# Pair 0 of a mixed, clamped low-rank linear layer as the plain product of four weight blocks

## The chip, the core and the metric

The kernel runs on one core of one Trainium2 chip. The metric is the device time of one execution in microseconds (us), as a median of several runs. TensorE (PE, with its weight loads as PEld) multiplies matrices, VectorE (DVE), ScalarE (ACT) and GpSimd (POOL) work elementwise, and SyncE (SP) and ScalarE issue the transfers (DMA) that appear here. SBUF is the memory on the chip, PSUM the banks in which TensorE sums.

## The reference

What is computed, with all inputs in float32:

```python
# x (128, 64, 1024), ids (128,), cond_w (16, 64, 64), W (1024, 1024), b (1024,)
# A (8, 1024, 16), Bm (8, 16, 1024), p (8,)
y = einsum('bct,bcd->bdt', x, cond_w[ids])          # one of 16 mixers for each batch row
z = einsum('bsd,od->bso', y, W) + b
u = einsum('bsd,edr->ebsr', y, A)
m = einsum('ebsr,ero,e->bso', u, Bm, p)
gamma = minimum(0.5 * norm(z) / (norm(m) + 1e-6), 1.0)   # norms over the last axis
return x + z + gamma * m
```

## The kernel before

Two batch rows of 64 channels fill the 128 partitions, which gives 64 tiles of 128 rows by 1024 columns, taken in 32 **pairs** (tile 2p is "r = 0", tile 2p + 1 is "r = 1"). The transposed W lies in four blocks of 512 by 512: W11 and W12 take the lower half of a tile's 1024 inputs, W21 and W22 the upper half, to the lower (1) or upper (2) half of the outputs.

**Precision.** Every operand of a large product is split in a high part (`..._hi`, a cast on ScalarE) and the rest (`..._lo`, a subtraction on VectorE), and a product of a tile half with a block is 4 chunks of 128 inputs times 3 passes (hi·hi, hi·lo, lo·hi): 12 matmuls of 512 columns. A "product" below means these 12.

**Seven products in place of eight.** For two tiles, four half-tile inputs and four blocks the plain way takes eight products. The kernel takes seven, by Strassen's scheme in Winograd's form: it needs sums of the inputs (S1 to S4, from the mixed tiles) and of the blocks:

```python
T1 = W12 - W11;  T2 = W22 - T1;  T3 = W22 - W12;  T4 = W21 - T2
```

T1 to T4 are made once, at the start, and split like W; W11, W21 and W22 are needed as they are. The results are put together again on VectorE with the bias (`bias_p1`, `make_u2`, `make_u3`, `make_z11`, `make_z12`, `make_z22`).

**What a pair is on TensorE**, in the steady loop (`step` at the end of the kernel): product W11 into bank b_ps; `down` (24 matmuls of 256 columns, the low-rank u); W21 onto b_ps, after `p1_biased`; `up(0)` (the low-rank m of tile 0); T4 into a_ps; T2 into b_ps; the next pair's tile 0 mixed (`mix`, with the mixers); T1 into c_ps; T3; the next tile 1 mixed; `up(1)`; W22 onto c_ps. The order on each engine is written out by hand; semaphores (`wait_ge`, `then_inc`) tie the engines together.

**Pair 0 before the change.** TensorE's order is the 12 warm-up matmuls on zeros (L818); mix tile 0; W11; mix tile 1; W21; `down`; T2; T1; T3; mix tile 2; W22; T4; mix tile 3; `up(1)`; and then pair 1 with W11. GpSimd makes S1, S4, the difference of the biases, and in chunks T1 (L350) and T3 (L355). VectorE makes T2 (L542) and T4 (L546) from them, one chunk after the other, and all the `_lo` parts of W (L535), y (L554), S (L575) and A (L654). ScalarE makes the `_hi` parts of W (L395), y (L400) and S (L413).

**Loads.** All are on SP's queue, in this order: ids, x tile 0, the two mixer squares of tile 0 (64 by 64 each, at an address read from the ids), W11 in 4 chunks, x tile 1, the mixers of tile 1, bias, W21, A, W12, W22, p, B, x tiles 2 and 3, and the mixers of these.

Of the kernel before, what the change touches and what calls it, by code (L numbers as in the profile page):

```python
# [5 lines left out]
def conditioned_clamped_low_rank_linear_kernel(  # L6
# [10 lines left out]
):  # L17

# [30 lines left out]
    W_ORDER = (W11, W21, T2, T1, T3, W22, T4)  # L49
# [7 lines left out]
    RAW11, RAW21, RAW12, RAW22 = range(4)  # L57
    w_blocks = [w[h * H:(h + 1) * H, o * H:(o + 1) * H].rearrange("(k p) o -> k p o", p=P)
                for h, o in ((0, 0), (1, 0), (0, 1), (1, 1))]

    ctx = ExitStack()
    with ctx:  # L62
# [45 lines left out]
        def stat(n, r):  # L108
# [6 lines left out]
        raw11 = w_hi_raw[:, T4, :, :]  # L115
        raw21 = w_lo_raw[:, T4, :, :]
        raw12 = w_lo_raw[:, T3, :, :]
        raw22 = w_lo_raw[:, W22, :, :]
        raw = [raw11, raw21, raw12, raw22]
        w_from = {W11: raw11, W21: raw21, W22: raw22, T3: raw12, T4: raw21,  # L120
                  T1: w_lo_raw[:, T1, :, :], T2: w_lo_raw[:, T2, :, :]}
# [15 lines left out]
        w_loaded = [[sem(f"w_loaded{n}_{k}") for k in range(HC)] for n in range(4)]  # L137
# [11 lines left out]
        w_lo_ready = sem("w_lo_ready")  # L149
        t1_made = sem("t1_made")  # L150
# [21 lines left out]
        u3_biased = sem("u3_biased")  # L172
# [55 lines left out]
        def _(sp):  # L228
# [13 lines left out]
            sp.dma_start(cond_ids[:, :], condition.rearrange("(o n) -> o n", o=1)).then_inc(ids_loaded, 16)  # L242
# [53 lines left out]
        def _(pool):  # L296
            def make_s1(p):

                pool.wait_ge(s2_made, p + 1)
                nc.gpsimd.tensor_tensor(s14[:, 0, :, :], s23[:, 0, :, :], s14[:, 0, :, :], ALU.add).then_inc(s1_made, 1)  # L300

            def make_s4(p):

                pool.wait_ge(s2_made, p + 1)
# [42 lines left out]
            for k in range(HC):  # L347
                pool.wait_ge(w_loaded[RAW11][k], 16)
                pool.wait_ge(w_loaded[RAW12][k], 16)
                nc.gpsimd.tensor_tensor(w_from[T1][:, k, :], raw12[:, k, :], raw11[:, k, :], ALU.subtract  # L350
                                        ).then_inc(t1_made, 1)
            for k in range(HC):
                pool.wait_ge(w_loaded[RAW22][k], 16)
                pool.wait_ge(t1_made, k + 1)
                nc.gpsimd.tensor_tensor(raw12[:, k, :], raw22[:, k, :], raw12[:, k, :], ALU.subtract  # L355
                                        ).then_inc(t3_made, 1)
# [26 lines left out]
        def _(act):  # L383
# [553 lines left out]
```

## Time and profile before

| | |
|---|---|
| median of 3 runs | 952.65 us (952.53 to 954.38) |
| the profiled execution: its own time | 954.46 us |
| the profiled execution: span of the core | 952.6 us |
| TensorE matmuls busy | 918.7 us, 96% of the span |
| VectorE, ScalarE, GpSimd busy | 61%, 38%, 36% of the span |
| granted TensorE clock, mean | 0.983 |

The 1.9 us between the span and the execution's own time lie around the program. "Granted clock" is the share of full speed that TensorE was given: 1.00 is its 2.4 GHz level and 0.50 its 1.2 GHz level. The page gives TensorE's share of each fortieth of the span (23.8 us each). The first fortieth has 6 tenths, the next three 5, 8 and 9, and all the others 9 or more but for the last with 5.

### The profile page before, as it was taken

How to read it: one execution, taken by the hardware profiler on the slowest of the kernel's cores; microseconds unless marked ns; L12 is line 12 of the kernel's file. 1: busy time of each engine (PE TensorE's matmuls, PEld its weight loads, DVE VectorE, ACT ScalarE, POOL GpSimd, SP SyncE). 2: the span in 40 equal slices, each digit the busy share in tenths (PEclk: the TensorE clock that was granted, in tenths of full speed). 3: DMA queues.
4: the chain of work that ended last, by engine and by line, in shares of the span. 5: the costliest groups of instructions: out<-in, count | busy, mean ns of one | idle time of the engine just before them, and what ended most of it. 6: DMA issues, size and time to landing. Idle time of an engine off the chain costs nothing. (4 is left out here: it accounts for less than half of the span.)

```text
span 952.6 us, 15191 instructions
## 1 busy us (share of the span) xinstructions
PE 918.7 (96%) x4876; PEld 789.8 (83%) x4876; DVE 583.6 (61%) x903; ACT 357.7 (38%) x704; POOL 346.1 (36%) x336
## 2 busy tenths in 40 slices
PE   6589999999999999999999999999999999999995
PEld 4478888888888888888888888888888888888883
DVE  4995566665556565556565556666555656555653
ACT  4353343434333434334334334343433343432431
POOL 2623344332244433234433234433224443323442
PEclk8699999999999999999999999999999999999998
DMA  8201222211222221122121122221122222112201
GB/s 260 78 23 69 92 92 69 91 65 48 91 91 76 84 87 47 70 91 91 69 91 45 67 91 91 69 91 67 48 88 91 81 79 90 45 69 91 92 23 66
DMA packets 32457, 75.17 MB, mean 79 GB/s; under 512 B 12729, under 2 KB 13754, under 8 KB 32442
## 3 DMA queue, kind: packets, MB, share of 16 engines
q1 hardware_dynamic: 32442, 74.99, 22.4%
q8 instruction: 7, 0.11, 0.0%
q14 instruction: 8, 0.07, 0.0%
HBM read 41.42 MB, written 33.55 MB: 79 GB/s over the span
## 5 line engine op out<-in xcount | busy, mean ns | idle before, releaser
L400 ACT CAST y_hi<-mix_ps 128x512 fp32r<-128x512 f32 x128 | 75.7, 591 | 322.9 <-PE mix_ps L739 322.9
L331 POOL TENSOR_TENSOR stats<-stats 128x1 f32<-128x1 f32 x32 | 17.7, 554 | 447.1 <-ACT squares L447 447.1
L575 DVE TENSOR_TENSOR s_lo<-s,s_hi 128x512 fp32r<-128x512 f32 x128 | 142.1, 1129 | 4.9 <-ACT s_hi L413 0.6
L317 POOL TENSOR_TENSOR z<-z,x_in 128x512 f32<-128x512 f32 x64 | 82.7, 1293 | 130.4 <-ACT squares L428 130.4
L739 PEld LDWEIGHTS mix_ps<-mixer,x_in 128*128 128x128 f32 x1024 | 124.0, 191 | 5.9 <-issue 1.0
L739 PE MATMUL mix_ps<-mixer,x_in 128*128 128x128 f32 x1024 | 124.6, 275 | 0.5 <-DMA mixer<-in_L_cond_weights_dram 0.5
L413 ACT CAST s_hi<-s 128x512 fp32r<-128x512 f32 x128 | 79.0, 618 | 114.3 <-POOL s L305 96.5
L554 DVE TENSOR_TENSOR y_lo<-mix_ps,y_hi 128x512 fp32r<-128x512 f32 x128 | 87.9, 687 | 53.9 <-ACT s L406 48.6
L752 PE MATMUL b_ps<-w_hi,y_hi 128*128 128x512 f32 x256 | 102.1, 399 | 7.9 <-DVE z L640 4.8
L752 PE MATMUL b_ps<-w_hi,s_hi 128*128 128x512 f32 x256 | 100.5, 392 | 9.4 <-DVE w_lo L535 9.4
L752 PE MATMUL c_ps<-w_hi,s_hi 128*128 128x512 f32 x256 | 102.4, 400 | 1.9 <-issue 1.8
L752 PE MATMUL b_ps<-w_lo,y_hi 128*128 128x512 f32 x256 | 101.3, 396 | 0.0
L752 PE MATMUL b_ps<-w_hi,y_lo 128*128 128x512 f32 x256 | 101.1, 395 | 0.0
L752 PE MATMUL b_ps<-w_lo,s_hi 128*128 128x512 f32 x256 | 100.3, 392 | 0.0
L752 PE MATMUL b_ps<-w_hi,s_lo 128*128 128x512 f32 x256 | 100.1, 391 | 0.0
L752 PE MATMUL c_ps<-w_lo,s_hi 128*128 128x512 f32 x256 | 99.8, 390 | 0.0
L752 PE MATMUL c_ps<-w_hi,s_lo 128*128 128x512 f32 x256 | 99.8, 390 | 0.0
L620 DVE TENSOR_TENSOR z<-b_ps,z 128x512 f32<-128x512 f32 x32 | 22.1, 692 | 111.6 <-PE b_ps L752 111.6
L707 DVE TENSOR_TENSOR z<-a_ps,bias 128x512 f32<-128x512 f32 x31 | 21.4, 692 | 107.2 <-PE a_ps L752 107.2
L311 POOL TENSOR_TENSOR z<-z,x_in 128x1024 f32<-128x1024 f32 x32 | 76.8, 2402 | 0.0
L785 PE MATMUL u_ps<-y_hi,a_hi 128*128 128x256 f32 x256 | 73.4, 287 | 0.6 <-DVE a_lo L654 0.6
L785 PE MATMUL u_ps<-y_lo,a_hi 128*128 128x256 f32 x256 | 73.3, 286 | 0.0
(92 smaller groups left out, 1835.7 us busy)
## 6 DMA issues: line engine op xcount, KB each, us to landing
x_in<-in_x_dram SPq DMA_DIRECT2D x64, 512.0 KB, 3.6
out_dram<-z SPq DMA_DIRECT2D x64, 512.0 KB, 2.7
w_lo_raw<-in_L_ffn_W_dram SPq DMA_DIRECT2D x12, 256.0 KB, 7.2
mixer<-in_L_cond_weights_dram SPq DMA_DIRECT2D x128, 16.0 KB, 2.1
w_hi_raw<-in_L_ffn_W_dram SPq DMA_DIRECT2D x4, 256.0 KB, 3.7
bias<-in_L_ffn_b_dram SPq DMA_DIRECT2D x1, 512.0 KB, 5.0
a_lo_raw<-in_L_ffn_A_dram SPq DMA_DIRECT2D x1, 512.0 KB, 7.3
b_lo_raw<-in_L_ffn_B_dram SPq DMA_DIRECT2D x1, 512.0 KB, 7.9
```

The lines of the kernel that those rows point to most:

```text
L311: nc.gpsimd.tensor_tensor(z1[:, :], z1[:, :], x_in[:, slot, :], ALU.add).then_inc(residual1_ready, 1)
L317: nc.gpsimd.tensor_tensor(z0[:, par, cols], z0[:, par, cols], x_in[:, 2 * par, cols], ALU.add).then_inc(residual0_ready, 1)
L331: nc.gpsimd.tensor_tensor(stat(NORM_Z, 1), stat(Z_SQ, 1), half, ALU.pow).then_inc(norm_z_ready[1], 1)
L400: nc.scalar.copy(y_part(y_hi, r, h), mixed(h)).then_inc(y_hi_ready, 1)
L413: nc.scalar.copy(s_hi[:, n, :, :], s_raw(n)).then_inc(s_hi_ready, 1)
L554: nc.vector.tensor_tensor(y_part(y_lo, r, h), mixed(h), y_part(y_hi, r, h).bitcast(fp32), ALU.subtract).then_inc(y_lo_ready, 1)
L575: nc.vector.tensor_tensor(s_lo[:, n, :, :], s_raw(n), s_hi[:, n, :, :].bitcast(fp32), ALU.subtract).then_inc(s_lo_ready, 1)
L620: nc.vector.tensor_tensor(z1[:, up_], b_ps[:, :], z0[:, par, up_], ALU.add).then_inc(u3_ready, 1)
L707: nc.vector.tensor_tensor(z1[:, lo], a_ps[:, :], bias[:, 2, :], ALU.add).then_inc(p4_biased, 1)
L739: made = nc.tensor.matmul(mix_ps[:, h, k * P:(k + 1) * P], x_in[:, slot, (h * HC + k) * P:(h * HC + k + 1) * P], mixer[:, r, :], start=Tru ...
L752: summed = nc.tensor.matmul(bank[:, :], left[:, k, :], right[:, n, k, :], start=(start and k == 0 and i == 0), stop=(k == HC - 1 and i == ...
L785: summed = nc.tensor.matmul(u_ps[:, 0:2 * P], left[:, k, :], right[:, k, :], start=(k == 0 and n == 0), stop=(k == KC - 1 and n == 2))
```

## The change

Pair 0 is no longer computed with seven products, but with the eight plain ones, straight from W11, W12, W21 and W22, which all have their splits made as they arrive. The new function `plain` runs one of them for tile r and half h, and counts in `plain_done`. Tile 0 goes to b_ps and c_ps, tile 1 to a_ps and the first half of m_ps. S1 to S4 of pair 0 and their splits are gone, and so is the recombination: VectorE adds the bias to four banks.

T1 to T4 are first used in pair 1. VectorE makes all of them, in instructions of 1024 columns (two chunks, `chunks`), in the order T3, T1, T2, T4, with the four bias additions between them; their splits (`split_t`) are of 1024 columns too, in the order T4, T2, T1, T3, and stand in VectorE's and ScalarE's order among the work on pair 0's end and pair 1's inputs. GpSimd keeps the difference of the biases and nothing else of that.

The ids and the mixers of tiles 0 and 1 are issued by ScalarE, ahead of its first cast. SP issues x tiles 0 and 1, then W11, W12, W21, A, W22, bias, p, B, x tiles 2 and 3, and only then waits for the ids, for the mixers of tiles 2 and 3. GpSimd clears the mixers before the zeros of the warm-up. The loop from pair 2 on is the same but for counts that start one lower.

```diff
@@ SP
-            sp.dma_start(cond_ids[:, :], ...)
-            sp.dma_start(x_in[:, 0, :], x_tiles[0]).then_inc(x_loaded[0], 16)
-            sp.wait_ge(ids_loaded, 16)
-            sp.wait_ge(mixer_zeroed, 1)
-            load_mixer(0, 0)
-            load_w(RAW11)
-            sp.dma_start(x_in[:, 1, :], x_tiles[1]).then_inc(x_loaded[1], 16)
-            load_mixer(1, 1)
+            for r in range(2):
+                sp.dma_start(x_in[:, r, :], x_tiles[r]).then_inc(x_loaded[r], 16)
+            load_w(W11)
+            load_w(W12)
+            load_w(W21)
+            sp.dma_start(a_raw, ...)
+            load_w(W22)
@@ GpSimd
-            make_s1(0)
-            make_s4(0)
...
-            for k in range(HC):
-                nc.gpsimd.tensor_tensor(w_from[T1][:, k, :], raw12[:, k, :], raw11[:, k, :], ALU.subtract
-            for k in range(HC):
-                nc.gpsimd.tensor_tensor(raw12[:, k, :], raw22[:, k, :], raw12[:, k, :], ALU.subtract
@@ ScalarE
+            act.dma_start(cond_ids[:, :], ...)
+            act.wait_ge(ids_loaded, 16)
+            act.wait_ge(mixer_zeroed, 1)
+            for r in range(2):
+                load_mixer(r, r)
...
+            split_w(W22)
+            square_z11(0, 0, True)
             split_u(0, True)
+            split_t(T4)
             act.wait_ge(bm_scaled, 1)
             nc.scalar.copy(b_hi[:, :], b_raw).then_inc(b_hi_ready, 1)
+            for h in range(2):
+                split_y(2, 0, h)
+                copy_y(1, h, True)
+            split_t(T2)
+            for h in range(2):
+                split_y(3, 1, h)
+            square_z1(0, True)
+            split_t(T1)
+            square_m1(0, True)
+            split_t(T3)
@@ VectorE
+            def make_t3():
+                for g in range(2):
+                    nc.vector.tensor_tensor(chunks(raw_t[T3], g), chunks(raw22, g), chunks(raw12, g), ALU.subtract
+                                            ).then_inc(t3_made, 1)
...
+            make_t3()
+            dve.wait_ge(plain_done, 5)
+            nc.vector.tensor_tensor(z0[:, 0, lo], b_ps[:, :], bias[:, 0, :], ALU.add).then_inc(z11_ready, 1)
+            make_t1()
+            dve.wait_ge(plain_done, 6)
+            nc.vector.tensor_tensor(z1[:, lo], a_ps[:, :], bias[:, 0, :], ALU.add).then_inc(z21_ready, 1)
+            make_t2()
+            make_t4()
...
+            split_t(T4)
...
+            split_y(1, 0, 0)
+            dve.wait_ge(plain_done, 8)
+            nc.vector.tensor_tensor(z1[:, up_], m_ps[:, lo], bias[:, 1, :], ALU.add).then_inc(z22_ready, 1)
+            split_y(1, 0, 1)
+            split_t(T2)
             split_y(1, 1, 0)
-            make_s3(1, False)
+            make_s3(1, True)
             split_y(1, 1, 1)
-            make_s2(1, False)
+            make_s2(1, True)
+            split_t(T1)
+            split_t(T3)
@@ TensorE
+            def plain(bank, r, h, n):
+                product(bank, y_part(y_hi, r, h), y_part(y_lo, r, h), n, h == 0, h == 1, r == 0, True
+                        ).then_inc(plain_done, 1)
...
+            for r, bank in ((0, b_ps[:, :]), (1, a_ps[:, :])):
+                y_ready(r, 0)
+                plain(bank, r, 0, W11)
+            for r, bank in ((0, c_ps[:, :]), (1, m_ps[:, lo])):
+                plain(bank, r, 0, W12)
+            for r, bank in ((0, b_ps[:, :]), (1, a_ps[:, :])):
+                y_ready(r, 1)
+                plain(bank, r, 1, W21)
             down()
...
+            plain(c_ps[:, :], 0, 1, W22)
+            for h in range(2):
+                mix(0, 2, h)
+            plain(m_ps[:, lo], 1, 1, W22)
             mix_next_1(0, 0, 0)
```

On **VectorE**, from the end of pair 0 to the bias addition that lets TensorE start pair 1's W21 (`bias_p1`, the addition into z from b_ps and bias). Before, w_lo is the low part of a block, y_lo that of a mixed tile, s a sum S2 or S3:

```order
L535 TENSOR_TENSOR w_lo<-w_lo_raw,w_hi 128x512 x4
L679 TENSOR_TENSOR b_lo<-b_lo_raw,b_hi 128x1024
L554 TENSOR_TENSOR y_lo<-mix_ps,y_hi 128x4x128 x2
L683 TENSOR_TENSOR z<-a_ps,z 128x512
L554 TENSOR_TENSOR y_lo<-mix_ps,y_hi 128x4x128
L562 TENSOR_TENSOR s<-s,mix_ps 128x512
L554 TENSOR_TENSOR y_lo<-mix_ps,y_hi 128x4x128
L570 TENSOR_TENSOR s<-mix_ps,s 128x512
L630 TENSOR_TENSOR z<-c_ps,z 128x512
L575 TENSOR_TENSOR s_lo<-s,s_hi 128x512
```

The same place after the change (L587 is the split of a T, L617 that of S2; the three small ones are the clamp's factor, L649 adds the low-rank part of tile 1, L682 is `bias_p1`):

```order
L612 TENSOR_TENSOR s<-mix_ps,s 128x512
L587 TENSOR_TENSOR w_lo<-w_lo_raw,w_hi 128x1024 x4
L617 TENSOR_TENSOR s_lo<-s,s_hi 128x512
L629 TENSOR_SCALAR stats<-stats 128x1
L632 RECIPROCAL stats<-stats 128x1
L635 TENSOR_SCALAR stats<-stats 128x1
L649 SCALAR_TENSOR_TENSOR z<-m_ps,stats,z 128x1024
L682 TENSOR_TENSOR z<-b_ps,bias 128x512
```

The splits of T1 and T3, which stood before pair 0's last products, stand now behind pair 1's S2 and ahead of `bias_p1`.

On **ScalarE**, the first instructions of the program. Before:

```order
L472 ACT_TABLE_LOAD
L472 ACTIVATE stats<-stats 128x1
L400 CAST y_hi<-mix_ps 128x4x128
L406 COPY s<-mix_ps 128x512
L400 CAST y_hi<-mix_ps 128x4x128
L406 COPY s<-mix_ps 128x512
L395 CAST w_hi<-w_hi_raw 128x512 x4
```

After the change, of which the start is shown (the lines from L384 to L385 come four times in all, two for each tile):

```order
L481 DMA cond_ids<-in_itok_B_15_dram 1x128
L483 ACT_TABLE_LOAD
L483 ACTIVATE stats<-stats 128x1
L384 TENSOR_LOAD cond_ids
L384 ISA x2
L385 ISA
L385 DMA mixer<-in_L_cond_weights_dram 64x64
```

The mixers' transfers stand ahead of the first cast, and the two copies of tile 0 (L406) are gone.

## Rows read from the trace of the kernel before

**Rows 1.** Busy time by stretch (us:us length, PE, PEld, DVE, ACT, POOL, clock, DMA)
```profile
123.60:152.20 28.60, 28.60 (x156) 24.73 (x155) 17.47 (x28) 10.62 (x21) 10.59 (x11) 1.00 0.21 76
```

**Rows 2.** Waits of TensorE, first 95 us (waiter, releaser: total us, times, longest)
```profile
PE b_ps L752 <- DVE w_lo L535: 9.6, 2, 9.4
PE b_ps L752 <- DVE z L640: 4.8, 2, 3.5
PE b_ps L752 <- ACT w_hi L395: 2.7, 1, 2.7
```

**Rows 3.** Timeline, TensorE (start us, us, engine, line, out<-in, count, idle before)
```profile
6.56 2.02 PE L739 MATMUL mix_ps<-mixer,x_in 128*128 128x128 f32 x16 [0.51 <-DMA mixer<-in_L_cond_weights_dram]
11.32 0.47 PE L752 MATMUL b_ps<-w_hi,y_hi 128*128 128x512 f32 x1 [2.73 <-ACT w_hi L395]
...
15.74 1.95 PE L739 MATMUL mix_ps<-mixer,x_in 128*128 128x128 f32 x16
...
42.31 0.77 PE L752 MATMUL b_ps<-w_hi,s_hi 128*128 128x512 f32 x1 [9.37 <-DVE w_lo L535]
...
65.08 0.39 PE L752 MATMUL b_ps<-w_hi,y_hi 128*128 128x512 f32 x1
...
67.80 0.28 PE L785 MATMUL u_ps<-y_hi,a_hi 128*128 128x256 f32 x1
...
72.17 0.50 PE L752 MATMUL b_ps<-w_hi,y_hi 128*128 128x512 f32 x1 [1.35 <-DVE z L640]
...
75.07 0.61 PE L796 MATMUL m_ps<-b_hi,u_hi 128*128 128x512 f32 x2
...
76.43 0.39 PE L752 MATMUL a_ps<-w_hi,y_hi 128*128 128x512 f32 x1
```

**Rows 4.** Busy time by stretch, columns as in rows 1
```profile
12.00:15.00 3.00, 3.00 (x9) 2.33 (x8) 0.98 (x2) 0.00 (x0) 0.00 (x0) 0.50 0.95 246
...
43.00:45.00 2.00, 2.00 (x6) 1.53 (x5) 2.00 (x4) 2.00 (x6) 0.00 (x0) 0.50 0.00 0
46.00:54.00 8.00, 7.89 (x42) 6.42 (x41) 7.98 (x14) 5.12 (x10) 0.00 (x0) 1.00 0.00 0
...
6.00:24.00 18.00, 11.03 (x51) 8.43 (x50) 10.34 (x15) 9.36 (x17) 3.92 (x3) 0.85 0.99 317
```

**Rows 5.** Timeline of SP's queue, issues
```profile
0.71 0.36 SPq L242 DMA_DIRECT2D cond_ids<-in_itok_B_dram  x1
...
3.24 1.84 SPq L233 DMA_DIRECT2D mixer<-in_L_cond_weights_dram  x2
```

**Rows 6.** The mixers' 8 transfers of the first 30 us, issue to landing
```profile
DMA to landing us min/median/max: 1.8/4.6/8.2
```

**Rows 7.** Timeline, VectorE and GpSimd, subtractions of blocks and splits in pair 0
```profile
32.24 6.72 POOL L355 TENSOR_TENSOR w_lo_raw<-w_lo_raw 128x512 f32<-128x512 f32 x4
...
34.43 1.74 DVE L542 TENSOR_TENSOR w_lo_raw<-w_lo_raw 128x512 f32<-128x512 f32 x1
...
41.48 4.90 DVE L535 TENSOR_TENSOR w_lo<-w_lo_raw,w_hi 128x512 fp32r<-128x512 f32 x8
...
53.36 0.75 DVE L670 TENSOR_SCALAR b_lo_raw<-b_lo_raw,stats 128x1024 f32<-128x1024 f32 x1
...
59.45 1.22 DVE L679 TENSOR_TENSOR b_lo<-b_lo_raw,b_hi 128x1024 fp32r<-128x1024 f32 x1
```

**Rows 8.** Timeline, pair 1: ScalarE, GpSimd and VectorE up to bias_p1
```profile
64.38 1.06 ACT L447 ACTIVATE squares<-z 128x1024 bf16<-128x1024 f32 x1
...
66.13 2.40 POOL L311 TENSOR_TENSOR z<-z,x_in 128x1024 f32<-128x1024 f32 x1
...
67.28 1.80 DVE L575 TENSOR_TENSOR s_lo<-s,s_hi 128x512 fp32r<-128x512 f32 x1 [0.57 <-ACT s_hi L413]
...
69.47 1.29 POOL L300 TENSOR_TENSOR s<-s 128x512 f32<-128x512 f32 x1
...
69.53 0.16 DVE L587 TENSOR_SCALAR stats<-stats 128x1 f32<-128x1 f32 x1 [0.45 <-POOL stats L336]
...
71.44 0.68 DVE L640 TENSOR_TENSOR z<-b_ps,bias 128x512 f32<-128x512 f32 x1
```

More of the change, by code:

```diff
@@ L48, in conditioned_clamped_low_rank_linear_kernel @@
     W11, W21, W22, T1, T2, T3, T4 = range(7)
-    W_ORDER = (W11, W21, T2, T1, T3, W22, T4)
+    W12 = T4
+    W_ORDER = (W11, W12, W21, W22)
+    T_ORDER = (T4, T2, T1, T3)
     S1, S2, S3, S4 = range(4)
@@ L55, in conditioned_clamped_low_rank_linear_kernel @@
     out_tiles = out.rearrange("(n q) c t -> n (q c) t", q=PER)
-    RAW11, RAW21, RAW12, RAW22 = range(4)
-    w_blocks = [w[h * H:(h + 1) * H, o * H:(o + 1) * H].rearrange("(k p) o -> k p o", p=P)
-                for h, o in ((0, 0), (1, 0), (0, 1), (1, 1))]
+    w_blocks = {n: w[h * H:(h + 1) * H, o * H:(o + 1) * H].rearrange("(k p) o -> k p o", p=P)
+                for n, h, o in ((W11, 0, 0), (W12, 0, 1), (W21, 1, 0), (W22, 1, 1))}
     ctx = ExitStack()
@@ L114, in conditioned_clamped_low_rank_linear_kernel @@
         idle = squares[:, lo]
[L115 to L121, printed above, removed]
+        raw11 = w_hi_raw[:, T1, :, :]
+        raw12 = w_lo_raw[:, T1, :, :]
+        raw21 = w_hi_raw[:, T3, :, :]
+        raw22 = w_lo_raw[:, T2, :, :]
+        raw = {W11: raw11, W12: raw12, W21: raw21, W22: raw22}
+        raw_t = {T1: raw12, T2: raw22, T3: w_lo_raw[:, T3, :, :], T4: raw21}
         a_raw = a_lo_raw[:, :, :]
@@ L136, in conditioned_clamped_low_rank_linear_kernel @@
         out1_stored = sem("out1_stored")
-        w_loaded = [[sem(f"w_loaded{n}_{k}") for k in range(HC)] for n in range(4)]
+        w_loaded = {n: [sem(f"w{name}_{k}_loaded") for k in range(HC)]
+                    for n, name in ((W11, "11"), (W12, "12"), (W21, "21"), (W22, "22"))}
         ids_loaded = sem("ids_loaded")
@@ L523, in _, with split_w @@
         def _(dve):
[L524 to L526 removed]
+            def split_w(n):
+                for k in range(HC):
                     dve.wait_ge(w_hi_ready, w_count(n, k))
[L528 to L536 removed]
@@ new lines, in split_t @@
+            def split_t(n):
+                for g in range(2):
+                    dve.wait_ge(t_hi_ready, t_count(n, g))
+                    if n == T2:
+                        dve.wait_ge(t4_made, g + 1)
+                    elif n == T1:
+                        dve.wait_ge(t2_made, g + 1)
+                    nc.vector.tensor_tensor(chunks(w_lo[:, n, :, :], g), chunks(raw_t[n], g),
+                                            chunks(w_hi[:, n, :, :], g).bitcast(fp32), ALU.subtract
+                                            ).then_inc(t_lo_ready, 1)
@@ L694, in step @@
                         continue
-                    make_z12(p - 1, 1 - j)
+                    if not first:
+                        make_z12(p - 1, 1 - j)
                     split_s(p, S2)
@@ L742, in mix, with product @@
                 made.then_inc(mix_done, 1)
[L744 removed]
+            def product(bank, hi, lo_, n, start=True, stop=True, w_arrives=False, group_open=False):
                 for k in range(HC):
```

269 lines of the change are left out of this document (122 added, 147 removed).

## The prediction

> **What bounds the kernel now.** I read the busy time by stretch first. In a steady pair TensorE is busy 28.60 of 28.60 us at full clock [rows 1], and the list of its waits names none after the first pair and a bit. The change leaves the loop as it is, so nothing can be won or lost there, and the question is only how early pair 1 gets going. The list of TensorE's waits in the first 95 us [rows 2] says what the start costs: 9.6 us behind the low parts of the T blocks, 4.8 us behind `bias_p1`, 2.7 us behind the first casts. The timeline then gives the places [rows 3]: the first product starts at 11.32, T2 at 42.31 after 9.37 us of nothing, pair 1's W11 at 65.08. TensorE also runs at half clock after such gaps: 0.50 from 12 to 15 us, after a gap of 2.73, and 0.50 again at 43 to 45, after the 9.37 [rows 3, 4].
>
> I use one milestone for both kernels, the start of **pair 1's T4 product**, at 76.43 before [rows 3]. From there on the orders are the same and TensorE is full, so what the milestone moves, the end moves.
>
> **Prices.** A product at full clock is 67.80 - 65.08 = 2.72 us. The `down` is 2.9 (67.80 to 72.17 less the 1.35 of idle). An `up` is 76.43 - 75.07 = 1.36, a mixed tile 1.9 to 2.0 [rows 3]. The first product, which met the half clock, took 15.74 - 11.32 = 4.42, so one fall of the clock costs 1.6 us or so. On VectorE a 512-wide split is 4.90/8 = 0.61 and a 1024-wide one 1.22 [rows 7], in a row I take 1.19 (the row's number holds a tail that overlaps the next one).
>
> **Part 1, the loads.** Before, the ids are issued at 0.71 and the first mixer at 3.24; two take 1.84 with their address reads, so they come about 1.3 apart [rows 5]. ScalarE does the same from the same time: issues at about 3.3, 4.6, 5.9 and 7.3. Landing took 1.8 at best, 4.6 in the median and 8.2 at worst for the eight of the first 30 us [rows 6]; the long ones stood behind big loads on the same queue. On ScalarE's queue nothing stands ahead of them, but SP keeps the transfers busy with x and W. No row shows a mixer beside another queue's load, so the bounds are 1.8 and 8.2. I take 2.1, near the lower end, because what was ahead of the slow ones in their own queue is not ahead here. Tile 0 is then mixed at 6.5, as before (6.56), and tile 1's mixers land at 9.3; mixing it ends at 11.1. The **first product starts at 11.1**, against 11.32, and this time the gap ahead of it is under a microsecond, so that it need not meet the half clock.
>
> The weights must keep up. From 6 to 24 us 317 GB/s moved [rows 4]. Up to W22 there are 5.8 MB, which takes 18.2 us from about 2.3 on: W22 is in at 20.5, while TensorE wants it at 30 and VectorE at about 20. This edit costs nothing with that cover; if the rate fell to the 246 GB/s of 12 to 15 us, W22 would be 5 us later, and VectorE some 4.
>
> The Trainium skill speaks against this part: "DMA: Bandwidth & Descriptors", section Rules for kernel authors, says that spreading transfers over issuing engines gains no bandwidth, since they share the same 16 engines. The section on queues, rings and completion order adds that each engine takes turns between queues, packet by packet. By that the mixers share with W rather than queue behind it, which is the side I took; nothing in the trace of before has two queues at work, so no run here shows it yet.
>
> **Part 2, TensorE's pair 0.** Eight products for seven adds 2.72. From 11.1: six products to 27.4, `down` to 30.3, W22 for tile 0 to 33.0, tile 2 mixed to 34.9, W22 for tile 1 to **37.6**. No wait for a T is left in it, which is where the 9.37 us go. But the next thing, mixing tile 3, needs tile 2's low parts, and those stand late in VectorE's order.
>
> **Part 3, VectorE becomes the bound.** Its work from the first y split at 8.3 (an estimate: half of tile 0's mix after 6.5, and a cast): 20 splits of 512 (4 of y, 16 of W) are 12.2, A 1.2, T3 2.4, and one instruction of GpSimd's (below) 1.2, which is 25.3; with small gaps 25.7. Product 5 ended at 24.7, so VectorE is not waiting. Then z11 0.61, T1 2.4, a second one of GpSimd's 1.2, z21 0.6, T2 and T4 4.8, the scaling of B 0.7 [rows 7], u's 256 columns 0.35 (by half of a split's), z12 0.6, T4's splits 2.4, B's 1.2, tile 2's first half 0.6: **41.1**. TensorE idles from 37.6 to 41.1, and by the rows above meets the half clock: mixing tile 3 takes 3.6 in place of 1.9, to 44.8. `up(1)` to 46.2, pair 1's W11 to 48.9, `down` to **51.7**. There it waits for `bias_p1`.
>
> **Part 4, what stands ahead of `bias_p1`.** VectorE has T2's splits, two of y, S3 and S2 until 47.1. Then T1's and T3's splits, 4.8, S2's 0.6, the small ones and the add of m (69.53 to 71.44, 1.9) and `bias_p1` 0.7 [rows 8]: 8.0, so 55.1 if nothing interferes. GpSimd does. Rows of before show how: while it subtracts blocks, its four take 6.72 (1.7 each) and VectorE's one takes 1.74 where 0.61 is its own price [rows 7]; and a split met by the 2.40 of the residual takes 1.80 [rows 8]. Each waits for the other's whole instruction, so one of GpSimd's 512-wide ones between two of VectorE's costs 1.7 - 0.6 = 1.1 to 1.29, I take 1.2. In pair 0 and 1 these come: the residual of tile 1 (2.40) starts when its squares are in, at 46.9 (ScalarE's last cast of y ends 0.7 after the mix, at 45.5, and the squares take 1.06 and a read of the sum [rows 8], with a small one of GpSimd's about 0.5 more before the residual), and holds VectorE until 49.8, that is 2.7; then S1, the second half of tile 0's residual, and S4, 3.7 together. 55.1 + 2.7 + 3.7 = **61.5**.
>
> "SBUF — State Buffer", section SBUF: two separate sides, in the Trainium skill, calls this an exclusive lock, held for a whole instruction, against VectorE's instructions with two SBUF inputs. The trace agrees (1.74 against 0.61), and bandwidth shared by halves would cost VectorE about 0.6 for each instead of 1.2, which would end this part some 3 us sooner.
>
> So TensorE idles 9.8 us at 51.7, now behind `bias_p1`, where it idled 1.35 before. W21 meets the half clock and takes 2.72 + 1.6 = 4.3, to 65.9, `up(0)` to **67.3**: T4 starts, its splits long there. Against 76.43 that is 9.1 us. What is late next: T2 wants S2's split and z11, which are ready; T1 and T3 have theirs by 58; tile 0's x of the next pair is loaded by 66 and wanted at 72. None waits.
>
> **The sum.** 76.43 - 67.3 = 9.1. The profiled execution took 954.46 (span 952.6), so it would take 945.4; against the median 952.65 it is **943.5**, my forecast.
>
> **The rivals.**
>
> A: *GpSimd's instructions don't get in between.* If VectorE keeps its turn where both want it, the 3.7 go, and with a shorter gap in part 3 the clock may hold there. 943.5 - 3.7 = 939.8, or 938.2 with 1.6 for the clock. For it: in pair 1 before, VectorE's way to `bias_p1` met three of GpSimd's and lost 1.2 once [rows 8]. Against it: rows 7.
>
> B: *the mixers land late* beside SP's loads. At the median of 4.6, tile 0 is mixed at 9.2 in place of 6.5; VectorE, the bound, moves with it by 2.7, and the clock falls in the gap for some 0.6 more: 946.8. At the worst, 8.2, it is 7 us: 950.5.
>
> C, the other side, *the mixers wait for the whole load.* If both queues were served as one in order of size or place, tile 0's second mixer would come with W22, at 20.4 in place of 6.5: 13.9 later, 957.4. It decides from a landing 9.1 us later than I assume, at 15.6. The longest landing seen, 8.2, would be at 12.8.
>
> D: *the change doesn't do what it says*, the time stays: the milestone would have to sit behind something I don't see, such as loads of W at 246 GB/s and B together: 943.5 + 4 + 3.3 = 950.8.
>
> **Chances.** Forecast (941.5 to 945.5) 0.58, A 0.18, B 0.17, C 0.03, D 0.04. The range from 938.5 to 948.0 holds the forecast, A and the likelier part of B. Differences under 0.2% (1.9 us) are about what a measurement of this kernel can't tell from none. Faster by more: forecast, A, most of B, half of D, 0.94. Same 0.03, slower 0.03.
>
> **What will show it.** Right: the first product at about 11 at full clock; TensorE nearly full to 37; two gaps, of 3 to 4 us ahead of tile 3's mix, released by y_lo, and of 8 to 10 ahead of pair 1's W21, released by VectorE's z; VectorE's splits of T1 and T3 taking over 1.2 beside GpSimd; T4 of pair 1 at 67. Wrong: mixers landing over 3 us after issue; TensorE waiting for w_hi or w_lo in pair 0 (the loads); a second gap under 6 us (A); any idle after the milestone.

## The result and the profile after

| | before | after |
|---|---|---|
| median | 952.80 us (952.53 to 954.38, 4 runs) | 945.95 us (945.04 to 947.43, 4 runs) |
| ratio | | 0.9917 (95%: 0.9901 to 0.9933) |
| profiled execution, its span | 952.6 us | 943.2 us |
| mean granted clock | 0.983 | 0.991 |
| pair 1's T4 product starts | 76.43 us | 67.42 us |

The forecast was 943.5 us with a range of 938.5 to 948.0. The time lies in the range and 2.45 us above the forecast. The milestone came out at 67.42 us against a forecast of 67.3. That looks like a hit; the sections below show that two errors of over 4 us cancelled in it, and why the medians differ by 6.85 us while the spans of the two profiled executions differ by 9.4.

TensorE's waits in the first 95 us after the change (waiter, releaser: total us, times, longest), to be set beside [rows 2]:

```profile
PE b_ps L789 <- DVE z L682: 6.4, 1, 6.4
PE mix_ps L776 <- DMA mixer<-in_L_cond_weights_dram: 3.4, 1, 3.4
PE mix_ps L776 <- DVE y_lo L596: 2.6, 2, 2.2
```

The 9.6 us behind the low parts of the T blocks are gone. In their place stand three shorter waits: for the mixers of tile 0, for tile 2's low parts ahead of tile 3's mix, and for `bias_p1` (L682) ahead of pair 1's W21. The timeline of TensorE has the places, columns as in [rows 3]:

```profile
10.71 4.61 PE L776 MATMUL mix_ps<-mixer,x_in 128*128 128x128 f32 x24 [3.39 <-DMA mixer<-in_L_cond_weights_dram]
...
16.60 0.47 PE L789 MATMUL b_ps<-w_hi,y_hi 128*128 128x512 f32 x1
...
45.52 2.26 PE L776 MATMUL mix_ps<-mixer,x_in 128*128 128x128 f32 x16 [2.19 <-DVE y_lo L596]
...
61.17 0.80 PE L789 MATMUL b_ps<-w_hi,y_hi 128*128 128x512 f32 x1 [6.42 <-DVE z L682]
...
67.42 0.39 PE L789 MATMUL a_ps<-w_hi,y_hi 128*128 128x512 f32 x1
```

Tile 0 is mixed at 10.71 where it was 6.56, the first product starts at 16.60 where it was 11.32 [rows 3], and from there TensorE has no gap until 43.33, which is 45.52 less the 2.19.

VectorE in pair 0, and GpSimd's difference of the biases beside it (start us, us, engine, line, out<-in, count, idle before):

```profile
13.23 0.69 DVE L596 TENSOR_TENSOR y_lo<-mix_ps,y_hi 128x512 fp32r<-128x512 f32 x1 [13.23 <-ACT y_hi L410]
...
21.55 2.50 DVE L546 TENSOR_TENSOR w_lo<-w_hi_raw,w_hi 128x512 fp32r<-128x512 f32 x4
...
31.19 3.44 DVE L560 TENSOR_TENSOR w_lo_raw<-w_lo_raw,w_hi_raw 128x1024 f32<-128x1024 f32 x2
...
44.69 0.68 DVE L596 TENSOR_TENSOR y_lo<-mix_ps,y_hi 128x512 fp32r<-128x512 f32 x1
...
51.15 6.87 DVE L587 TENSOR_TENSOR w_lo<-w_lo_raw,w_hi 128x1024 fp32r<-128x1024 f32 x4
...
60.44 0.68 DVE L682 TENSOR_TENSOR z<-b_ps,bias 128x512 f32<-128x512 f32 x1
```

```profile
21.58 9.44 POOL L352 TENSOR_TENSOR bias<-bias 128x512 f32<-128x512 f32 x1 [19.62 <-DMA bias<-in_L_ffn_b_dram]
32.11 1.44 POOL L326 TENSOR_TENSOR z<-z,x_in 128x512 f32<-128x512 f32 x1 [1.10 <-ACT squares L438]
```

The four splits from 21.55 take 2.50 together, their own price [rows 7 has 0.61 each], while an instruction of GpSimd's that took 1.4 to 1.7 in some kernels below stretches over 9.44 us beside them. VectorE paid for one of GpSimd's (T1, 3.44 where two alone take 2.35), not for two. From 13.23 to 61.12 it is idle twice, 1.01 us at 14 and 0.72 at 30; so everything ahead of `bias_p1` is one chain of VectorE's. It starts 2.52 us behind the start of tile 0's mix, where the kernel with early mixers below (`e1_mixers_sp`) takes 1.78 (6.59 to 8.37), because the two mixes ran at half clock behind their gap of 3.39 us (us:us length, PE, PEld, DVE, ACT, POOL, clock, DMA share and GB/s):

```profile
12.00:14.00 2.00, 2.00 (x11) 1.99 (x10) 0.69 (x1) 0.58 (x1) 0.00 (x0) 0.50 1.05 390
```

### The profile page after: what moved, and what is told of

Read it like the earlier page. It is cut to its first block and busy times, and to the rows that moved or that the text cites. A ratio compares the mean times of both kernels' runs of the same rounds, so it can differ in the third digit from the quotient of the medians.

```text
span 943.2 us, 15151 instructions
## 1 busy us (share of the span) xinstructions
PE 917.3 (97%) x4888; PEld 790.1 (84%) x4888; DVE 571.8 (61%) x889; ACT 355.5 (38%) x694; POOL 338.9 (36%) x326
## 5 line engine op out<-in xcount | busy, mean ns | idle before, releaser
L617 DVE TENSOR_TENSOR s_lo<-s,s_hi 128x512 fp32r<-128x512 f32 x124 | 134.3, 1103 | 4.2
L776 PE MATMUL mix_ps<-mixer,x_in 128*128 128x128 f32 x1024 | 126.7, 277 | 6.0 <-DMA mixer<-in_L_cond_weights_dram 3.4
L423 ACT CAST s_hi<-s 128x512 fp32r<-128x512 f32 x124 | 76.6, 618 | 114.2 <-POOL s L314 97.9
L789 PE MATMUL c_ps<-w_hi,s_hi 128*128 128x512 f32 x248 | 99.1, 400 | 0.0
L789 PE MATMUL c_ps<-w_lo,s_hi 128*128 128x512 f32 x248 | 96.7, 390 | 0.0
L789 PE MATMUL c_ps<-w_hi,s_lo 128*128 128x512 f32 x248 | 96.6, 389 | 0.0
L789 PE MATMUL b_ps<-w_hi,s_hi 128*128 128x512 f32 x248 | 96.5, 389 | 0.0
L789 PE MATMUL b_ps<-w_lo,s_hi 128*128 128x512 f32 x248 | 96.5, 389 | 0.0
L789 PE MATMUL b_ps<-w_hi,s_lo 128*128 128x512 f32 x248 | 96.5, 389 | 0.0
L828 PE MATMUL u_ps<-y_hi,a_lo 128*128 128x256 f32 x256 | 72.4, 283 | 0.0
```

The lines of the kernel that those rows point to most:

```text
L423: nc.scalar.copy(s_hi[:, n, :, :], s_raw(n)).then_inc(s_hi_ready, 1)
L617: nc.vector.tensor_tensor(s_lo[:, n, :, :], s_raw(n), s_hi[:, n, :, :].bitcast(fp32), ALU.subtract).then_inc(s_lo_ready, 1)
L776: made = nc.tensor.matmul(mix_ps[:, h, k * P:(k + 1) * P], x_in[:, slot, (h * HC + k) * P:(h * HC + k + 1) * P], mixer[:, r, :], start=Tru ...
L789: summed = nc.tensor.matmul(bank, left[:, k, :], right[:, n, k, :], start=(start and k == 0 and i == 0), stop=(stop and k == HC - 1 and i ...
L828: summed = nc.tensor.matmul(u_ps[:, 0:2 * P], left[:, k, :], right[:, k, :], start=(k == 0 and n == 0), stop=(k == KC - 1 and n == 2))
```

## Experiments

All ran beside the kernel before; its median in these was 953.5 to 953.7 (952.57 to 956.43). The column "behind T4" is the span less the start of pair 1's T4 product.

| kernel | median us (runs) | T4 at | span | behind T4 |
|---|---|---|---|---|
| before, first profile | 952.80 | 76.43 | 952.6 | 876.17 |
| b_again | 953.37 (952.53 to 956.23) | 78.14 | 954.3 | 876.16 |
| after, first profile | 945.95 | 67.42 | 943.2 | 875.78 |
| a_again | 946.12 (945.31 to 946.82) | 68.41 | 944.2 | 875.79 |
| e1_mixers_sp | 945.90 (945.59 to 946.32) | 68.66 | 944.5 | 875.84 |
| e5_hold_w | 946.02 (945.21 to 946.33) | 68.18 | 944.0 | 875.82 |
| e7_w_first | 945.26 (944.60 to 945.78) | 68.00 | 943.8 | 875.80 |
| e10_y_first | 945.84 (945.31 to 946.64) | 68.54 | 944.4 | 875.86 |
| e2_pool_later | 944.62 (944.45 to 944.79) | 67.16 | 943.0 | 875.84 |
| e3_bias_first | 938.36 (937.82 to 939.81) | 58.67 | 936.0 | 877.33 |
| e9_bias_u2 | 937.88 (937.81 to 938.20) | 60.37 | 936.2 | 875.83 |
| e8_all | 935.87 (935.66 to 936.31) | 58.69 | 934.5 | 875.81 |
| e11_all_y | 934.47 (933.84 to 935.81) | 56.86 | 932.7 | 875.84 |

The last column is the reason why one milestone serves for all: behind T4 each profiled execution takes 875.8 us, but for e3, where TensorE waits once more. The kernel before takes 0.38 more, in the tail behind the last product. There GpSimd's small instruction ends ahead of VectorE's last `add_m1` in one kernel and beside it in the other: VectorE starts 0.52 after that instruction's start before (942.83 and 943.35) and 0.15 after it now (933.83 and 933.98).

### Both kernels once more: what varies

> The kernel before once more, unchanged, for its profiled execution. If the executions of one kernel differ by where the granted clock falls (theory), this one shows pair 1's T4 product of before again near 76.4 us, and a span that differs from 952.6 by the time at lower clock after 75 us: near 951 if the profiled one before was a slow one of its kind. If the difference of 1.8 us between that execution and the median came from the start instead (rival), T4 lies near 74.6 and the rest is unchanged.

> The changed kernel once more, unchanged, for its profiled execution. Median again 945.9 (945 to 947.5). Theory (what varies lies behind 75 us): pair 1's T4 product again within 0.5 us of 67.4, whatever the span is. Rival (the start varies as the mixers land earlier or later): T4 between 66 and 69, and the span moves with it.

Both theories fell, and the rivals were right in that all of the difference lies ahead of T4. (The rival's own number for the kernel before, 74.6, didn't come: this execution was slower still, at 78.14.) But it isn't the mixers. Those of tiles 0 and 1 landed alike in the two executions of the kernel after (5.5/6.0/6.5 and 5.5/5.8/6.2 us at least, in the median and at most), and tile 2's low parts were out at the same time (44.69 and 44.65). The windows of the granted clock show it (us:us length, PE, PEld, DVE, ACT, POOL, clock, DMA). First the kernel after, then the same once more, right behind the gap of 2.19 us that both have ahead of tile 3's mix:

```profile
47.00:49.00 2.00, 2.00 (x14) 1.75 (x13) 2.00 (x3) 1.45 (x3) 0.00 (x0) 1.00 0.03 8
```

```profile
47.00:49.00 2.00, 2.00 (x10) 1.90 (x10) 2.00 (x3) 0.84 (x2) 0.00 (x0) 0.50 0.03 8
```

With the fall, mix and `up` together take 4.87 us up to pair 1's W11 (45.47 to 50.34), without it 3.48 (45.52 to 49.00): 1.4 us, of which 1.0 is left at T4. It doesn't get there on TensorE's own row, which has a wait of 6 us further on to take it up. The late mix delays ScalarE's last cast and the squares of tile 1, so GpSimd's residual starts 0.93 us later and stands for longer in the way of VectorE's first split of T1. First the kernel after, then the same once more:

```profile
50.05 2.41 POOL L320 TENSOR_TENSOR z<-z,x_in 128x1024 f32<-128x1024 f32 x1
51.15 2.39 DVE L587 TENSOR_TENSOR w_lo<-w_lo_raw,w_hi 128x1024 fp32r<-128x1024 f32 x1
```

```profile
50.98 2.40 POOL L320 TENSOR_TENSOR z<-z,x_in 128x1024 f32<-128x1024 f32 x1
51.35 3.11 DVE L587 TENSOR_TENSOR w_lo<-w_lo_raw,w_hi 128x1024 fp32r<-128x1024 f32 x1 [0.16 <-ACT w_hi L405]
```

Of the residual 1.31 us were left when the split began in the one, and 2.03 in the other; the split, 1.2 by itself, took 1.2 and 1.9 more. So it waited for the rest of the instruction that was running.

The kernel before has a gap of 1.78 us in its first profile and of 2.14 in this one, at 56 us. In the first the clock behind it was 1.00, in this one

```profile
56.00:60.00 4.00, 3.53 (x9) 2.81 (x10) 4.00 (x6) 1.85 (x4) 1.26 (x1) 0.58 0.00 0
```

The product behind it took 4.42 us (56.47 to 60.89) in place of 2.83, which is 1.6 of the 1.7 by which T4 differs. So the two first profiles weren't at the same point of their spreads. The first profile of before, at 954.46, was 1.8 us slower than its median, and that of after, at 945.04, was the fastest of its four.

### Where the mixers' time goes

```diff
 SP
+            sp.dma_start(cond_ids[:, :], ...)
             for r in range(2):
                 sp.dma_start(x_in[:, r, :], x_tiles[r])...
+            sp.wait_ge(ids_loaded, 16)
+            sp.wait_ge(mixer_zeroed, 1)
+            for r in range(2):
+                load_mixer(r, r)
             load_w(W11)
 ScalarE
-            act.dma_start(cond_ids[:, :], ...)
...
-            for r in range(2):
-                load_mixer(r, r)
```

> The changed kernel with one part of it undone: SP issues the ids, x tiles 0 and 1, then waits for the ids and issues the four mixer transfers of tiles 0 and 1, and only then W11 and the rest. ScalarE issues nothing. Theory 1 (the mixers landed late because their transfers shared the DMA engines with SP's x and W): they land about 2 us after issue, tile 0 is mixed from 6.5 (10.7 in the changed kernel), the first product starts at 11 to 12 in place of 16.6, and since VectorE is the bound from there, pair 1's T4 product comes 3 to 4.5 earlier, near 63.5, and the time falls by the same, to about 942. Rival: VectorE or the loads of W, which start 5 us later here, take it back, and T4 of pair 1 stays within 1 us of 67.4.

The landing of tile 0's and 1's mixers, issue to landing, first in the kernel after (ScalarE's queue, beside x and W), then here (SP's queue, behind x and ahead of W):

```profile
DMA to landing us min/median/max: 5.5/6.0/6.5
```

```profile
DMA to landing us min/median/max: 2.0/2.1/2.7
```

Tile 0 was mixed at 6.59 here, 4.1 us sooner, and the time was the same, 945.90. Most of the gain went into W11. It is issued at 7.43, behind the four mixers (4.31 us of issues), so its casts wait for each chunk, the first product crawls from 11.76 and the second begins at 16.99, where the kernel after has its first at 16.60. TensorE is still 2.3 us ahead there, but the bound is VectorE. Its chain began 4.9 us sooner; it waited for the chunks of W11 and was 2.0 ahead behind them (15.97 in place of 17.95). GpSimd's difference of the biases, which got in here, took 1.1 (T3 is 3.44 in place of 2.36), and at tile 2's first split 0.74 was left (43.95). The rest went behind TensorE's gap, which is now 3.83 us:

```profile
44.77 3.75 PE L776 MATMUL mix_ps<-mixer,x_in 128*128 128x128 f32 x16 [3.83 <-DVE y_lo L596]
```

The clock fell there (0.50 from 47 to 49 us), the splits of T1 and T3 took 7.62 with a wait of 0.68 ahead of them, and T4 came at 68.66. So the early mixers were paid for by the late W11; what they are worth beside an early one no run shows.

```diff
 SP
+            sp.wait_ge(ids_loaded, 16)
             load_w(W11)
```

> The changed kernel, but SP issues x tiles 0 and 1 and then waits for the ids before it issues W11, so that W and the mixers are issued at the same time, on two queues. Theory 1 as a matter of turns between queues: the mixers still share the engines with W and land 4 us or more after issue, if a little sooner than the 5.3 to 7.6 of the changed kernel; tile 0 is mixed at 8.5 to 10. Theory 2 (what delays them is only the backlog that SP had queued before them): they land within 3 us, tile 0 is mixed before 8, and the time falls by 3 us.

W11 was issued at 2.48, and the mixers, issued from 3.40, still landed in 5.0, 6.3 (median) and 6.5 us. Theory 2, under 3 us, is out as it was put. But the edit changed little: W11's head start over the mixers is 0.92 us here and was 1.25 (1.64 to 2.89) in the kernel after, so it doesn't tell a share of the engines from a backlog of W.

The packets of the kernel after say where the time goes. The first mixer is issued at 2.89. These are the queues (packets, MB, share of 16 engines) from 3 to 7 us, where ScalarE's queue q10 has no row, and from 7 to 12:

```profile
q1 hardware_dynamic: 416, 1.10, 83.5%
```

```profile
q1 hardware_dynamic: 1000, 1.81, 98.2%
q10 hardware_dynamic: 320, 0.07, 6.5%
```

For over 4 us after the issue nothing of the mixers moves, although the engines aren't full (83.5%); once they move, they go among W's packets. In e1 the first pair landed in 2.0 to 2.7 us with x running at 385 GB/s ahead of it (3 to 5 us), so busy engines alone aren't the cause. In the kernel before tile 1's mixers stood behind W11 and x tile 1 on SP's queue and landed within 3.6 us, so W11 ahead of them alone isn't either. What holds back the first packet here no run shows. The mean over 6 to 24 us is 368 GB/s in the kernel after and 317 in the kernel before [rows 4].

### W11's splits in the idle time

```diff
 ScalarE and VectorE, pair 0
+            split_w(W11)
             for h in range(2):
                 split_y(0, 0, h)
-            split_w(W11)
...
 VectorE
+            make_t1()
             dve.wait_ge(bias_loaded, 16)
...
-            make_t1()
```

> The changed kernel with W11's casts and splits ahead of tile 0's y in pair 0, on ScalarE and VectorE both, and T1 made ahead of z11 on VectorE. Theory: in the changed kernel VectorE idles until 13.2 us for tile 0's y, which waits for the late mixers, while W11 is already in (its chunks land 6.2 to 8). So W11's four splits (about 5 us with their waits) go into that idle time, VectorE's chain starts some 2 us earlier, the gap of 2.2 us ahead of tile 3's mix closes, and pair 1's T4 product starts at 65.4 instead of 67.4: 944.0. Rival (VectorE's chain isn't what delays the second half of the stage, its GpSimd turns are): the start comes earlier, but T4 stays at 67.4 and the time at 945.9.

VectorE began at 8.64 with W11's splits, that is 2.5 us of work before the mixed tile was there, and tile 2's first y split was at 44.70, where the kernel after had it at 44.69. The theory missed what would take the place of the saved time. VectorE's timeline in this kernel:

```profile
15.31 0.69 DVE L596 TENSOR_TENSOR y_lo<-mix_ps,y_hi 128x512 fp32r<-128x512 f32 x1 [1.01 <-ACT y_hi L410]
...
20.89 3.60 DVE L546 TENSOR_TENSOR w_lo<-w_hi_raw,w_hi 128x512 fp32r<-128x512 f32 x4
...
34.22 3.29 DVE L568 TENSOR_TENSOR w_lo_raw<-w_lo_raw 128x1024 f32<-128x1024 f32 x2
```

```profile
21.80 1.53 POOL L352 TENSOR_TENSOR bias<-bias 128x512 f32<-128x512 f32 x1 [19.85 <-DMA bias<-in_L_ffn_b_dram]
```

It now waits for two more y casts (0.75 and 0.43) behind the 1.01 that both kernels have, and both of GpSimd's 512-wide instructions cost it a turn: 3.60 for four splits that took 2.50, and 3.29 for two that took 2.34. The same GpSimd instruction gets in at once and takes 1.53 instead of 9.44. Over all the profiles it was held for 9.4 to 10.3 us in eight and through in 1.4 to 1.7 in three. e8 and e11 below have the same orders up to there, and it was through in one (1.41) and held in the other (10.31), so the orders alone don't decide it. The median, 945.26, is 0.7 under the kernel after's first one and within that one's spread (945.04 to 947.43); T4 at 68.00 lies between its two profiles, as the rival had it.

### The gap ahead of tile 3's mix

```diff
 VectorE (and ScalarE's b_hi moved behind tile 2's y casts)
-            split_t(T4)
+            split_y(1, 0, 0)
+            split_t(T4, (0,))
+            split_y(1, 0, 1)
             dve.wait_ge(b_hi_ready, 1)
             nc.vector.tensor_tensor(b_lo[:, :], ...)
-            split_y(1, 0, 0)
             dve.wait_ge(plain_done, 8)
             nc.vector.tensor_tensor(z1[:, up_], m_ps[:, lo], ...)
-            split_y(1, 0, 1)
+            split_t(T4, (1,))
```

> The changed kernel with tile 2's y splits taken ahead of T4's splits and of b_lo on VectorE (and ahead of b_hi on ScalarE), so that TensorE's 2.2 us idle ahead of tile 3's mix goes (mix at 43.3 instead of 45.5). Theory (pair 1's W21 waits for VectorE's chain up to bias_p1, whose length is unchanged): the gap only moves, W21 then waits 8.6 instead of 6.4, pair 1's T4 product stays at 67.4 to 68.4: 945.9. Rival (each idle stretch of TensorE before it counts for itself): T4 2.2 earlier, 943.8.

```profile
43.25 1.05 PE L777 MATMUL mix_ps<-mixer,x_in 128*128 128x128 f32 x8
...
61.83 0.80 PE L790 MATMUL b_ps<-w_hi,y_hi 128*128 128x512 f32 x1 [7.22 <-DVE z L682]
```

The gap went and tile 3 was mixed 2.3 us sooner. The time stayed, 945.84: the idle time reappeared ahead of W21, 7.22 us instead of 6.42, with 0.67 and 0.84 at two other places. This shows that in the kernel after it is VectorE's chain up to `bias_p1`, and not TensorE's own gaps, that sets T4.

### GpSimd's turns beside T1's and T3's splits

```diff
 GpSimd
                         norm_m(p - 1, 1)
+                        if first:
+                            pool.wait_ge(t_lo_ready, t_count(T3, 1))
                         make_s1(p)
```

> The changed kernel, but GpSimd starts on pair 1's S1 (and what stands behind it, the second half of tile 0's residual and S4) only when VectorE has made the last split of T3. The prediction's theory (GpSimd and VectorE take turns, one instruction each): the four 1024-wide splits of T1 and T3, 6.87 us in the changed kernel, fall to about 5.5, bias_p1 comes over 1 us sooner, and so does pair 1's T4. Rival (VectorE, with its instructions back to back, hardly yields; what it lost was the residual of 1024, which stands ahead of S1): the four splits stay at 6.5 to 6.9 and bias_p1 at 60.4, give or take 0.5; the time is that of the changed kernel or up to 2 us more, because S1 is late.

The four splits take 5.79 here and 6.87 in the kernel after, and S1 comes behind them. The four begin at 51.7; GpSimd's row of S1, held back until they are done:

```profile
57.58 1.65 POOL L309 TENSOR_TENSOR s<-s 128x512 f32<-128x512 f32 x1 [3.07 <-DVE w_lo L589]
```

Alone the four take 4.7, so the residual and one small instruction cost 1.1 and S1 with the other small ones 1.1 more. The median fell by 1.3. Turns are taken, then, but all of them together cost 2.2 us here, where the prediction had 6.4.

### The place of `bias_p1`

```diff
 VectorE, end of pair 0's order
             make_s2(1, True)
-            split_t(T1)
-            split_t(T3)
+            bias_p1(1, 1)
...
 VectorE, step, pair 1 only
-                    split_s(p, S2)
                     make_gamma(p - 1, 1)
                     add_m1(p - 1)
-                    bias_p1(p, j)
+                    split_s(p, S2)
+                    make_z11(p, j)
+                    split_t(T1)
                     for n in (S3, S1, S4):
                         split_s(p, n)
-                    make_z11(p, j)
+                    split_t(T3)
```

> The changed kernel with another order on VectorE in pair 1 alone: bias_p1 stands right behind S2, ahead of the splits of T1 and T3; then the clamp's factor and the add of tile 1's m, S2's split, z11, T1's splits, the splits of S3, S1 and S4, and T3's splits. The theory that TensorE's 6.4 us of idle ahead of pair 1's W21, and the half clock behind them, are the price of the place of bias_p1: W21 starts at about 54.7, when down has ended, without idle and at full clock; T4 of pair 1 at 59 to 60 in place of 67.4, and the time 6 to 8 us less, near 938.5. Rival: the next thing is late in its place (up(0) waits for the add of m, or T1's product for its splits, or T3's), and 3 us or more of it come back as idle later in pair 1.

```profile
51.69 0.28 PE L836 MATMUL u_ps<-y_hi,a_hi 128*128 128x256 f32 x1
...
54.56 0.40 PE L797 MATMUL b_ps<-w_hi,y_hi 128*128 128x512 f32 x1
...
58.67 0.39 PE L797 MATMUL a_ps<-w_hi,y_hi 128*128 128x512 f32 x1
...
70.04 0.47 PE L797 MATMUL b_ps<-w_hi,s_hi 128*128 128x512 f32 x1 [1.25 <-DVE z L656]
```

W21 follows `down` without a gap and at full clock, so both the 6.4 us of waiting and the half clock behind them go, and T4 is at 58.67, 8.75 sooner. One new wait of 1.25 comes at 70.04, for `make_u2` (L656), which stood behind T3's splits. The median is 938.36, 7.6 us under the kernel after: as much as the change itself brought (6.85 in the first comparison, 7.4 in the second), from an order that the change brought in when it put the splits of T1 and T3 ahead of `bias_p1`.

### The parts put together

> The version with pair 1's bias_p1 right behind its product, and u2 made right behind T3's splits, without the move of W11's splits. Theory: TensorE's wait of 1.25 us for u2 at 70 us goes, so the time behind T4 is 875.8 instead of 877.3: 938.36 - 1.5 = 936.9, if the 2.5 us between that version and the one with both edits (935.87) came half from W11's splits. Rival (W11's splits moved into VectorE's idle time bring nothing, since the work displaced comes back as waits for y and turns with GpSimd): 935.9, the same as with both.

> The previous edit together with the bias of pair 1 taken right behind the S2 product's arrival, ahead of the splits of T1 and T3 (the version with that alone ran in 938.36), and with u2 made right behind T3's splits, which takes out the 1.25 us for which TensorE waited there for u2. Theory: the three gains are in a row and add up: 938.4 - 1.25 - 2.0 = 935.1. Rival (W11's split in the idle time brings nothing once W21's operand is early, since the gap ahead of tile 3's mix has its own cause): 937.1.

> The same order of tile 2's y splits in the version of 935.87, where bias_p1 stands right behind its product and VectorE had 0.7 us idle ahead of it. Theory: there TensorE's own row of products sets pair 1's T4, so the idle 1.83 us ahead of tile 3's mix counts: T4 at 56.9 instead of 58.7, 934.1; by what VectorE can't make up (0.7 idle plus what it does ahead of bias_p1) the gain may stop at 0.7: 935.1 for the rival.

e9 is e3 with `make_u2` behind T3's splits. The wait at 70 us is gone (behind T4 875.83 in place of 877.33), yet the median fell by only 0.5. In all five of its executions the clock was 0.990 against 0.994 in three of e3's four, and the profile has the fall behind the gap of 2.19 us:

```profile
47.00:49.00 2.00, 2.00 (x9) 1.99 (x10) 2.00 (x3) 0.69 (x2) 0.00 (x0) 0.50 0.03 8
```

e8 adds the move of W11's splits. In its profile the gap is 1.83, the clock there stays at 1.00, and tile 3 is mixed from

```profile
45.49 2.26 PE L786 MATMUL mix_ps<-mixer,x_in 128*128 128x128 f32 x16 [1.83 <-DVE y_lo L596]
```

That is where e3 has it (45.47), and T4 is at 58.69 as in e3 (58.67). The gap is shorter because TensorE came to it later, not because VectorE was done sooner (44.66 and 44.64 for tile 2's first split). Of the 1.68 between e9's T4 and e8's, 1.49 is the clock and 0.19 an earlier start of tile 3's mix; by the profiles the move of W11's splits itself brings nothing. The medians are less plain: e8's is 2.0 under e9's and, with the 1.5 of u2 taken off e3's, 1.0 under that too. So a part of it may be the move's, by way of the clock or otherwise; that isn't shown. Both expectations had named other sums, since neither had the clock in it. Nor is it shown that the shorter gap is why the clock held; it held in e3 and in the kernel after behind 2.19 too.

e11 adds the order of tile 2's y splits to e8. Now no chain of VectorE's hides that gap, and it counts:

```profile
42.57 1.95 PE L787 MATMUL mix_ps<-mixer,x_in 128*128 128x128 f32 x16
...
56.86 0.39 PE L800 MATMUL a_ps<-w_hi,y_hi 128*128 128x512 f32 x1
```

T4 is at 56.86, as forecast to the tenth, and the median is 934.47, ratio 0.9795 (0.9779 to 0.9812) to the kernel before and 11.5 us under the kernel after. The same edit that was worth nothing in e10 is worth 1.4 here.

## The prediction, point by point

**What bounds, and the milestone: right.** TensorE is full behind T4 in every kernel, and the span follows T4 one for one.

**Part 1, the landing of the mixers: wrong.** Bounds of 1.8 and 8.2 were given and 2.1 was taken, because nothing stood ahead of the mixers in their own queue. They took 5.5 to 6.5. Tile 0's mix came at 10.71 in place of 6.5 and the first product at 16.60 in place of 11.1. Of the 5.5 us at the first product 4.2 are the landing and 1.3 the half clock in the two mixes, of which rival B had 0.6. The step that failed is the choice within the bounds: an empty queue of their own didn't bring the mixers in early while W was issued on the other. The Trainium skill's rule in "DMA: Bandwidth & Descriptors", section Rules for kernel authors, is that a second issuer gains no bandwidth. The trace agrees: 389 GB/s from 8 to 9 us with two queues at work, 414 from 10 to 11 us in the kernel before with one. By the section on queues, rings and completion order the engines take turns between queues. The packets from 7 to 12 us agree, where the mixers went among W's. But the delay is the 4 us before the first of them, of which neither the runs nor that rule give the reason; it stays open. Rival B's sum of 2.7 to 7 us holds the 4.2 us of the mix.

**Part 2: right** in its sum. From the first product to the end of pair 0 it took 43.33 - 16.60 = 26.7 where the forecast has 26.5. (The rows named for `down` give 3.02 us, not 2.9; in e3 it takes 2.87.) TensorE waited for no part of W.

**Part 3, VectorE as the bound: right in kind.** Its chain ran from 13.23 instead of 8.3 (+4.9), and its first half of tile 2 was out at 45.4 instead of 41.1 (+4.3), mainly because one of GpSimd's two turns wasn't taken. Of the 4.9, 4.2 are the mixers and 0.7 the half clock in the mix. TensorE came to the gap 5.7 us late and VectorE's splits 4.3, so the gap was 2.19 in place of 3.5. The half clock behind it came in one of the two profiles of this kernel.

**Part 4: the wait right, its size wrong.** From the end of pair 1's sums to `bias_p1`'s end VectorE took 61.12 - 51.15 = 10.0, where the prediction has 61.5 - 47.1 = 14.4. Of GpSimd's instructions the residual was taken at 2.7 and three others at 3.7; e2 and the four splits' 6.87 make it 1.1 and 1.1. The error is in having each of them cost VectorE a whole turn. The residual cost only what was left of it when the first split wanted in. Behind the splits VectorE had S2's split, which met only a small instruction of GpSimd's, and then small instructions and ones that read PSUM. Those weren't stretched beside the other two:

```profile
59.24 1.28 DVE L649 SCALAR_TENSOR_TENSOR z<-m_ps,stats,z 128x1024 f32<-128x1024 f32 x1
```

```profile
58.40 1.34 POOL L326 TENSOR_TENSOR z<-z,x_in 128x512 f32<-128x512 f32 x1
59.70 1.26 POOL L314 TENSOR_TENSOR s<-s 128x512 f32<-128x512 f32 x1
```

The add of the same size for tile 0 (L642) takes 1.28 at 71.65 us with GpSimd idle. "SBUF — State Buffer", section SBUF: two separate sides, of the Trainium skill, gives the lock against GpSimd to VectorE's instructions with two SBUF inputs or in a two-port mode, and not to these. By that and these rows only the residual and S1, which met the splits, should have been charged. So 4.2 of the 6.4 us weren't there: 2.6 of rival A's 3.7, and 1.6 of the residual, which rival A had left standing. The trace of before had it already, in the row of pair 1 that rival A named for itself.

**The sum: right by cancelling.** +4.9 from the mixers and the half clock behind them, -0.6 in pair 0, -0.2 until the splits, -4.4 in part 4, +0.4 for W21 and `up(0)`, which took 6.25 at half clock instead of 5.8, gives +0.1: 67.42 against 67.3.

**From the milestone to the time: wrong by 2.45.** The saving of 9.1 was read off one execution and taken from the median of others. A median run of before has a span of about 950.8; if it too takes 876.17 behind T4, as both profiled ones do, its T4 is at 74.6 and not 76.43. That is 1.8 of the miss. The eight executions of the kernel after have a median span of 944.3, so T4 at 68.5, 1.2 later than the forecast, and the shorter tail gives 0.4 back: 1.8 + 1.2 - 0.4 = 2.6 against 2.45. The prediction named the difference between the two (954.46 and 952.65) and took it as a constant, when the milestone already held it. That it is a fall of the clock is likely but not shown: no execution near the median was profiled, and the mean clock sorts the executions of before only loosely (0.986 at 952.57 us and at 956.12).

**Rivals C and D: out.** The mixers came 4 us late and not 14, and no load of W was waited for.

## What to carry to other kernels

When work is taken out of a start-up, write down the next engine's chain as one list and ask of each item whether anyone waits for it: here a 0.7 us bias addition stood behind 6.9 us of splits that nobody needed for 10 us more, and moving it was worth as much as the whole change. A gap ahead of a place that another engine's chain sets anyway is free (e10) as long as the clock holds behind it, and becomes worth its length once that chain is short (e11). Before a milestone is turned into a time, see where the profiled execution stands among the times of its kernel: two profiles of the kernel before were both slower than its median.

## What the runs showed of the hardware

- Four small transfers (16 KB each) on a second queue, issued about 1 us behind the first of the loads of W, took 5.0 to 6.5 us to land (e5 and the kernel after); in the kernel after no packet of theirs moved in the first 4 us. On the loading queue itself, issued ahead of W, they took 2.0 to 2.7.
- A split of VectorE's that met GpSimd's residual waited for the rest of it: 1.2 us where 1.31 were left, 1.9 where 2.03 were. Its add that reads PSUM took 1.28 us beside GpSimd and without it.
- A 512-wide GpSimd instruction with two SBUF inputs was held for 9.4 to 10.3 us beside VectorE's unbroken row of such instructions in eight profiles, at no cost to VectorE, and got in within 1.4 to 1.7 us in three, at a cost of 1.1 to VectorE each. I have no rule for which; it stays open.
- After the same idle time of TensorE (2.19 us) the granted clock fell to 0.50 in some profiles (a_again, e9) and stayed at 1.00 in others (the first of after, e2, e3, e5). It moves T4 by 1.0 us in a_again and 1.5 in e9, and it accounts for the difference between the two profiles of the kernel after.
